# One selection made in two halves, message parts stored as floats, and a zero fill that waits for the loads

## The chip, the cores and the metric

The kernel runs on one core of one Trainium2 chip. The metric is the device time of one execution in microseconds. Three timed runs of the kernel before took 9149.21, 9165.05 and 9166.55 us; the median is 9165.05 us. The core has five engines that run side by side and wait for each other only through semaphores: TensorE (PE in the rows; PEld is its weight load), VectorE (DVE), ScalarE (ACT), GpSimd (POOL) and SyncE (SP), which here only issues DMAs.

## The reference

Four graph layers over 12500 nodes of 64 features and 400000 edges, `dst` sorted. Each layer's result is added to `x` and normalised over the features:

```python
x = ln(x + relu(segment_sum((x @ W0)[src] * edge_weight[:, None], dst)))
# layer 1: y = x + segment_sum over i=src of f(edge_attr) * (x @ Wl.T + bl)[dst]
#          f(e) = silu(e @ Wf1.T + bf1) @ Wf2.T + bf2 ; y = layernorm(y) * gamma + beta
x = ln(x + layer1(x))
# layer 2: h = x + segment_sum(x[src], dst); relu(h @ W1 + b1) @ W2 + b2
x = ln(x + layer2(x))
# layer 3: deg of src, dinv = rsqrt(deg); segment_sum over src of dinv[src]*dinv[dst]*(x @ W3)[dst] + bias
x = ln(x + layer3(x))
```

So every layer gathers a row per edge, makes a message of it, and sums the messages by node. The values are float32.

## The kernel before, in words

**Gather and scatter as matmuls.** Nodes are cut into 98 source blocks of 128 (NS) and 49 destination windows of 256 (NW). A cell is a pair of window and block, and holds up to 128 edges. For a cell a "hot" matrix (128 nodes x 128 edges) picks the rows of a node table, and a selection matrix (edges x 256 nodes of the window, or x 128 nodes of the block) sums the messages by node. Both are made on VectorE by comparing a row or a pair of indices with a ramp (`iotab`). A float is carried as three bfloat16 parts: the whole, the rest, and the low part; for a message they lie in three float slots, and the matmul reads the upper two bytes of each slot (`upper_half`).

**Stages, in order.** (1) A first block loads constants, weights and `x`; ACT issues the zero fill of the first four windows of the buffer `edge_rows` in DRAM (16 DMAs, L150); all engines meet at the end of the block. (2) `node_stage(0)` makes the first table. (3) `fused`, the longest stage, does two things at once: it computes the edge filter of layer 1 and writes one row per edge to its cell of `edge_rows`, and it runs layer 0 for a window whose cells are already sorted. (4) `node_stage(1)`, `filter_pass` (layer 1), (5) `node_stage(2)`, `sum_pass` (layer 2), (6) `node_stage(3)`, `read_pass` (layer 3), and the last normalisation. Other functions (`far_...`) are skipped at run time with these inputs.

**A beat of `fused`.** `run_beats` runs 52 beats (0 to 51). A beat has 14 steps (GW). In the beats 0 to 47 each of 13 steps also handles a chunk of 5 x 128 edges: DVE ranks the edges within their cells (`carried`, `ranked`, `placed`, `onehot`), PE does the filter matmuls and the counts, ACT writes the rows, and POOL scatters them with 5 indirect DMAs of 128 rows (L794): 65 in a beat, 3125 in all. Beats 49 to 51 have no chunks, and beat 48 has one. From beat 3 on each step also does the layer: `first` (hot matrix, L872), `second` (the selection of 7 cells x 256 nodes, L567, called at L880), on PE `gather` (L983) and `scatter` (L998), on ACT `whole` (L1070: table row times edge weight, straight into the first float slot), on DVE `remainder` (L887) and `lowest` (L892). The order within a step is written out by hand, once for each engine; buffers are double, and each wait names the step whose buffer comes free. SP loads the `piece` tiles of a window (f_piece) only when all indirect DMAs of the beat before have landed.

**`filter_pass`** goes through the windows in runs of 7 (98 runs), cut into sets of 2, 2, 2 and 1 windows. For each set DVE does `whole_message` (L1808, gathered row times filter), `first` (L1787), `rest_of_message` (L1819), `second` (L1796) and `low_of_message` (L1827). PE gathers the next set before it scatters this one (L1891, L1904).

Of the kernel before, what the change touches and what calls it, by code (L numbers as in the profile page):

```python
# [7 lines left out]
ALU = mybir.AluOpType  # L8
# [4 lines left out]
P = 128  # L13
# [48 lines left out]
def build(nc, a, out):  # L62
    ctx = ExitStack()
    with ctx:
# [87 lines left out]
        with nc.Block() as block:  # L152
# [13 lines left out]
            @block.scalar  # L166
            def _(act):
                act.wait_ge(s_const.sem, 12)
                for w in range(LEAD):
                    for q in range(4):  # L170
                        clear_quarter(act, w, q)
# [388 lines left out]
        def cells(g):  # L560

            return g // GH, g % GH * CG
# [14 lines left out]
        def fused():  # L577

            fctx = ExitStack()
            with fctx:  # L580
# [98 lines left out]
                with nc.Block() as block:  # L679
# [124 lines left out]
                    def _(dve):  # L804
# [70 lines left out]
                        def second(w, g):  # L875
                            h, lo = cells(g)
                            dma_wait(dve, y_pair[h], w)
                            wait(dve, y_sum, w, g - 1, GW)
                            settle(dve)
                            selection(dve, ysel[g % 2], ypair[h], lo, WIN).then_inc(y_sel.sem, 1)  # L880

                        def remainder(w, g):
                            wait(dve, y_whole, w, g + 1, GW)
# [5 lines left out]
                        def lowest(w, g):  # L889
                            wait(dve, y_rest, w, g + 1, GW)  # L890
                            settle(dve)
                            dve.tensor_tensor(upper_halves(msg[g % 2], 2), msg[g % 2][:, :, 1, :], upper_halves(msg[g % 2], 1),  # L892
                                              ALU.subtract).then_inc(y_low.sem, 1)

                        def summed(w):
# [6 lines left out]
                        def beat(b, extract, layer, prepare):  # L902
                            n = chunks(b)
                            more = chunks(b + 1) if isinstance(b, int) else BC
                            for g in range(GW):
# [15 lines left out]
                                if g < n:  # L921
                                    placed(b, g, 0)
                                    if g + 1 < n:
                                        onehot(b, g + 1)
                                if layer:
                                    lowest(b - 3, g)
                                if g < n:
# [779 lines left out]
        def filter_pass(n):  # L1707
# [3 lines left out]
            with ectx:  # L1711
# [21 lines left out]
                with nc.Block() as block:  # L1733
# [47 lines left out]
                    def _(dve):  # L1781
# [40 lines left out]
                        def low_of_message(t, s):  # L1822
                            lo, hi = steps(s)
                            part = msg[:, SETS[s][0] * CG:SETS[s][1] * CG, :]
                            reach(dve, x_rest, t, hi)
                            settle(dve)
                            dve.tensor_tensor(upper_of(part[:, :, 2 * D:3 * D]), part[:, :, D:2 * D],  # L1827
                                              upper_of(part[:, :, D:2 * D]), ALU.subtract).then_inc(x_msg.sem, hi - lo)

                        def run(t, i, last=False):  # L1830
# [549 lines left out]
```

## Time and profile before

| | us |
|---|---|
| median of three runs | 9165.05 |
| profiled execution, its own time | 9224.61 |
| its span | 9222.8 |
| PE / PEld busy | 7601.7 / 6594.3 |
| DVE busy | 6859.9 |
| ACT busy | 5230.8 |
| POOL busy | 3390.7 |

Rows are read so. In a table of windows: stretch, its length, then for each engine the busy time and the number of instructions, the granted share of TensorE's clock, the DMA share and GB/s. In a list of lines: line, engine, operation, out<-in by name, shape, count, then busy us and mean ns of one, then the idle time before it with what ended it. A timeline row is start, length, engine, line and names. In the waits: who waited for whom, the total, how many times, the longest. Records of one engine's successive instructions may overlap by some 0.1 us.

### The profile page before, as it was taken

To read this page: it belongs to the slowest core of one execution; us is meant where nothing else is said; L and a number is where in the kernel's file an instruction comes from. 1 tells how busy PE (TensorE), PEld (TensorE's weight loads), DVE (VectorE), ACT (ScalarE), POOL (GpSimd) and SP (SyncE) were. 2 spreads that over 40 slices of the span, in tenths; PEclk is the share of its full clock that TensorE was granted. 3 is DMA by queue.
4 is the path that set the end of the run, shared out by engine and by line. 5 is a ranking of instruction groups with operands and counts; after the bars stand their busy time and mean duration, and the time that the engine had idled before them with its cause. 6 is when DMAs were issued, how large, how long until landed. Compare 5 with 4: busy or idle time off the path is not lost. (4 is left out here: it accounts for less than half of the span.)

```text
span 9222.8 us, 312807 instructions
## 1 busy us (share of the span) xinstructions
PE 7601.7 (82%) x101781; PEld 6594.3 (72%) x101781; DVE 6859.9 (74%) x13109; ACT 5230.8 (57%) x12664; POOL 3390.7 (37%) x3201
## 2 busy tenths in 40 slices
PE   6688888888888888887577777776599998799998
PEld 3466666666666666665477777775599998799998
DVE  3476676766766667666689999998888887677777
ACT  2344444444444444444467777775577776688887
POOL 5777777777777777776000000000000000000000
PEclk8899999999999999998899999998799999899999
DMA  4555555555555555554277777774233332466665
GB/s 151 162 157 177 163 173 167 157 177 164 172 170 153 177 164 172 169 155 143 62 185 184 184 186 185 181 185 130 85 129 131 129 127 93 80 129 130 129 130 110
DMA packets 889994, 1385.03 MB, mean 150 GB/s; under 512 B 385510, under 2 KB 738726, under 8 KB 877174
## 3 DMA queue, kind: packets, MB, share of 16 engines
q1 hardware_dynamic: 760470, 1100.18, 44.2%
q10 hardware_dynamic: 29376, 174.02, 5.2%
q0 software_dynamic: 100000, 109.00, 4.0%
q8 instruction: 75, 1.23, 0.1%
q14 instruction: 73, 0.60, 0.0%
HBM read 1086.88 MB, written 295.86 MB: 150 GB/s over the span
## 5 line engine op out<-in xcount | busy, mean ns | idle before, releaser
L794 POOL DMA_INDIRECT edge_rows<-f_rows,f_index x3125 | 3290.9, 1053 | 967.2 <-issue 926.4
L1070 ACT ACTIVATE f_msg<-ps,f_yew 128x64 f32<-128x64 f32 x4802 | 1056.8, 324 | 1435.3 <-PE ps L983 1361.0
L567 DVE TENSOR_TENSOR x_sel<-iotab,x_pairs 128x1792 bf16<-128x1792 bf16 (+1 forms) x1372 | 1174.5, 856 | 208.1 <-issue 198.1
L1319 PE MATMUL ps<-x_msg,x_sel 128*128 128x192 bf16 x9604 | 1186.5, 246 | 2.5 <-issue 2.2
L1673 ACT ACTIVATE x_msg<-ps 128x384 bf16<-128x384 f32 (+1 forms) x2744 | 1015.3, 457 | 202.1 <-PE ps L1605 195.5
L1346 ACT ACTIVATE x_msg<-ps 128x768 bf16<-128x768 f32 (+1 forms) x1029 | 906.7, 916 | 353.5 <-PE ps L1300 303.2
L998 PE MATMUL ps<-f_msg,f_ysel 128*128 128x192 bf16 x9604 | 991.0, 256 | 108.9 <-issue 108.8
L1891 PE MATMUL ps<-tab,x_hot 128*128 (+1 forms) x28812 | 957.7, 194 | 23.5 <-ACT x_hot L1952 8.1
L1891 PEld LDWEIGHTS ps<-tab,x_hot 128*128 128x128 bf16 x28812 | 929.5, 98 | 53.7 <-issue 47.1
L998 PEld LDWEIGHTS ps<-f_msg,f_ysel 128*128 128x128 bf16 x9604 | 845.5, 99 | 135.7 <-issue 118.9
L1605 PE MATMUL ps<-tab,x_hot 128*128 (+1 forms) x9604 | 921.1, 247 | 18.8 <-ACT x_msg L1673 7.8
L1300 PE MATMUL ps<-tab,x_hot 128*128 128x192 bf16 x4802 | 790.2, 247 | 138.4 <-DVE x_hot L1249 138.4
L1952 ACT ACTIVATE x_hot<-x_away,ones 128x1792 bf16<-128x1792 bf16 (+1 forms) x392 | 628.4, 1603 | 400.0 <-PE ps L1891 382.0
L1319 PEld LDWEIGHTS ps<-x_msg,x_sel 128*128 128x128 bf16 x9604 | 831.3, 98 | 6.7 <-issue 3.3
L1605 PEld LDWEIGHTS ps<-tab,x_hot 128*128 128x128 bf16 x9604 | 799.8, 98 | 43.9 <-issue 26.4
L851 DVE TENSOR_REDUCE f_best<-ps 128x5 int32<-128x490 f32 x625 | 418.3, 669 | 503.0 <-PE ps L1025 498.6
L841 DVE TENSOR_SCALAR f_total<-ps 128x98 f32<-128x98 f32 x625 | 162.1, 259 | 835.4 <-PE ps L1013 828.9
L1904 PE MATMUL ps<-x_msg,x_sel 128*128 128x193 bf16 x4802 | 492.8, 251 | 348.3 <-issue 348.3
L1476 DVE TENSOR_SCALAR x_hot<-x_row,iota 128x896 bf16<-128x896 bf16 x1372 | 560.0, 451 | 277.9 <-PE ps L1605 258.1
L1860 POOL TENSOR_TENSOR x_added<-x_kept 128x448 f32<-128x448 f32 x14 | 18.5, 1323 | 2017.6 <-ACT x_kept L1964 2017.6
L567 DVE TENSOR_TENSOR f_ysel<-iotab,f_ypair 128x1792 bf16<-128x1792 bf16 x686 | 743.7, 1084 | 19.2 <-PE ps L998 12.7
L282 PE MATMUL ps<-bias_b,onesb 3*128 3x320 bf16 x625 | 196.1, 314 | 600.1 <-ACT f_hT L279 599.9
(190 smaller groups left out, 13971.7 us busy)
## 6 DMA issues: line engine op xcount, KB each, us to landing
x_row<-edge_row_dst SPq DMA_DIRECT2D x588, 448.0 KB, 4.9
edge_rows<-zeros ACTq DMA_DIRECT2D x204, 833.0 KB
f_piece<-edge_rows SPq DMA_DIRECT2D x343, 476.0 KB
f_yrow<-edge_row_src SPq DMA_DIRECT2D x686, 224.0 KB
x_row<-edge_row_src SPq DMA_DIRECT2D x98, 1568.0 KB, 6.3
x_f<-edge_rows SPq DMA_DIRECT2D x294, 476.0 KB, 3.7
edge_rows<-f_rows,f_index POOLq DMA_INDIRECT x3125, 2.3
x_row<-edge_row_dst SPq DMA_DIRECT2D x196, 224.0 KB, 3.4
```

The source lines that it names most:

```text
L567: return dve.tensor_tensor(sel[:, :, :].rearrange("p c (e two) -> p c e two", two=2), iotab[:, 0:columns].rearrange("p (e two) -> p e two" ...
L794: pool.indirect_dma_start(out=rowbuf, out_offset=bass.IndirectOffsetOnAxis(ap=index[:, j:j + 1], axis=0), in_=rows[:, j, :], in_offset=Non ...
L998: i = pe.matmul(sums[m], ysel[g % 2][:, c, m * P:(m + 1) * P], parts, start=False, stop=g == GW - 1 and c == CG - 1 and m == 1)
L1070: i = act.activation(msg[g % 2][:, c, 0, :], got[g % 2][:, c * D:(c + 1) * D], ACT.Copy, scale=yew[h][:, lo + c:lo + c + 1])
L1300: i = pe.matmul(psb[p % RING][:, k * VW:(k + 1) * VW], hot[c // CG % 2][:, c % CG, :], tab3[:, c, :, :].rearrange("p k d -> p (k d)"), sta ...
L1319: i = pe.matmul(total[:, m * VW:(m + 1) * VW], sel[c // CG % 2][:, c % CG, m * P:(m + 1) * P], msg[:, p % RING, k, :, :].rearrange("p k d ...
L1346: act.activation(msg[:, lo:hi, :, :, :].rearrange("p b k q d -> p b (k q d)"), psum[:, lo * 512:hi * 512].rearrange("p (b e) -> p b e", e= ...
L1476: o = dve.tensor_scalar(hot[BUFFER[j % RUN]][:, m, :, :].rearrange("p c e -> p (c e)"), row[h][:, at, :], iota2[:, m:m + 1], None, ALU.is_ ...
L1605: o = pe.matmul(got[k][:, c % 2 * VW:(c % 2 + 1) * VW], hot[b][:, m, c, :], piece(e, m * VW, VW), start=m == 0, stop=m == 1)
L1673: act.activation(msg[BUFFER[j]][:, 2 * k:2 * k + cells_of(k), :].rearrange("p c e -> p (c e)"), got[k][:, 0:cells_of(k) * VW], ACT.Copy).t ...
L1891: o = pe.matmul(psb[b][:, c * D:(c + 1) * D], hot[:, b, m, c * P:(c + 1) * P], piece(e + (j - lo) * WROW, m * VW + k * D, D), start=m == 0 ...
L1952: act.activation(hot[:, b:e, 1, :], away[:, 0:hi - lo, :], ACT.Relu, bias=ones[:, 0:1], scale=-1.0)\
```

## The change

Three edits.

1. The selection of 256 columns in `fused` becomes two instructions of 128 columns; the second stands behind `placed(b, g, 0)` and `onehot(b, g + 1)`, which so come between the halves. The semaphore is raised by the second.
2. In `lowest` and in `low_of_message` the third part is written as a float into its whole slot, not as a bfloat16 into the slot's upper half. The matmul reads the same upper half as before.
3. ACT's first 16 zero fills wait for the loads (`s_load`) and for the weight and bias blocks (`s_diag`).

```diff
             @block.scalar
             def _(act):
                 act.wait_ge(s_const.sem, 12)
+                act.wait_ge(s_load.sem, 16 * len(loads))
+                act.wait_ge(s_diag.sem, 16 * (len(blocks) + PARTS))
                 for w in range(LEAD):
                     for q in range(4):
                         clear_quarter(act, w, q)
...
                             wait(dve, y_sum, w, g - 1, GW)
                             settle(dve)
-                            selection(dve, ysel[g % 2], ypair[h], lo, WIN).then_inc(y_sel.sem, 1)
+                            chosen(w, g, 0)
+
+                        def chosen(w, g, m):
+                            h, lo = cells(g)
+                            shape = [P, CG, P // 2, 2]
+                            i = dve.tensor_tensor(ysel[g % 2][:, :, m * P:(m + 1) * P].rearrange("p c (e two) -> p c e two", two=2),
+                                                  iotab[:, m * P:(m + 1) * P].rearrange("p (e two) -> p e two", two=2)
+                                                  .unsqueeze(1).to_broadcast(shape),
+                                                  ypair[h][:, lo:lo + CG, :].unsqueeze(2).to_broadcast(shape), ALU.is_equal)
+                            if m == 1:
+                                i.then_inc(y_sel.sem, 1)
...
-                            dve.tensor_tensor(upper_halves(msg[g % 2], 2), msg[g % 2][:, :, 1, :], upper_halves(msg[g % 2], 1),
+                            dve.tensor_tensor(msg[g % 2][:, :, 2, :], msg[g % 2][:, :, 1, :], upper_halves(msg[g % 2], 1),
                                               ALU.subtract).then_inc(y_low.sem, 1)
...
                                     placed(b, g, 0)
                                     if g + 1 < n:
                                         onehot(b, g + 1)
+                                if go:
+                                    chosen(*ahead, 1)
                                 if layer:
                                     lowest(b - 3, g)
...
-                            dve.tensor_tensor(upper_of(part[:, :, 2 * D:3 * D]), part[:, :, D:2 * D],
+                            dve.tensor_tensor(part[:, :, 2 * D:3 * D], part[:, :, D:2 * D],
                                               upper_of(part[:, :, D:2 * D]), ALU.subtract).then_inc(x_msg.sem, hi - lo)
```

On DVE, a step of a beat in `fused` before: f_ysel is the selection, f_hot the one-hot of source blocks, f_msg the message, f_slot and f_index the placing.

```order
L851 TENSOR_REDUCE f_best<-ps 128x5
L898 TENSOR_REDUCE acc<-ps 128x2x64
L567 TENSOR_TENSOR f_ysel<-iotab,f_ypair 128x1792
L859 TENSOR_SCALAR f_slot<-f_best 128x5
L833 TENSOR_TENSOR f_hot<-iotas,f_src_block 128x490
L892 TENSOR_TENSOR f_msg<-f_msg 128x7x64
L865 SCALAR_TENSOR_TENSOR f_index<-f_slot,f_cell 128x5
L872 TENSOR_SCALAR f_yhot<-f_yrow,iota 128x896
```

The same step now.

```order
L853 TENSOR_REDUCE f_best<-ps 128x5
L910 TENSOR_REDUCE acc<-ps 128x2x64
L887 TENSOR_TENSOR f_ysel<-iotab,f_ypair 128x7x128
L861 TENSOR_SCALAR f_slot<-f_best 128x5
L835 TENSOR_TENSOR f_hot<-iotas,f_src_block 128x490
L887 TENSOR_TENSOR f_ysel<-iotab,f_ypair 128x7x128
L904 TENSOR_TENSOR f_msg<-f_msg 128x7x64
L867 SCALAR_TENSOR_TENSOR f_index<-f_slot,f_cell 128x5
L874 TENSOR_SCALAR f_yhot<-f_yrow,iota 128x896
```

The selection is in two, f_slot and f_hot stand between its halves, and the message's low part stands behind the second half. (The reduce into acc is there in a beat's first step alone.)

On ACT, the first block before, with what each instruction waits for.

```order
L150 DMA edge_rows<-zeros 128x1666 [waits s_const]
L150 DMA edge_rows<-zeros 128x1666 x15
L152 UNCONDITIONAL_BRANCH
L533 UNCONDITIONAL_BRANCH [waits barrier_Pool_Activation_PE_DVE_SP_release]
L368 ACT_TABLE_LOAD
```

And now.

```order
L150 DMA edge_rows<-zeros 128x1666 [waits s_diag,s_load,s_const]
L150 DMA edge_rows<-zeros 128x1666 x15
L152 UNCONDITIONAL_BRANCH
L535 UNCONDITIONAL_BRANCH [waits barrier_Pool_Activation_PE_DVE_SP_release]
L370 ACT_TABLE_LOAD
```

All 16 DMAs now stand behind the wait, and behind them stands the branch by which ACT leaves the block, and then the barrier that all engines pass before the node stage.

## Rows read from the trace of the kernel before

**Rows 1.** Table of windows: the start, fused with POOL, its tail, filter pass.

```profile
0.00:40.00 40.00, 0.08 (x1) 0.11 (x2) 2.79 (x13) 0.12 (x1) 11.17 (x23) 1.00 0.86 349
64.00:4334.00 4270.00, 3521.44 (x36786) 2671.16 (x36784) 2771.57 (x6979) 1797.57 (x7369) 3290.93 (x3126) 0.91 0.54 163
4334.00:4515.00 181.00, 107.44 (x1789) 101.34 (x1789) 138.69 (x226) 85.92 (x391) 0.15 (x1) 0.94 0.44 125
...
4625.00:6410.00 1785.00, 1393.47 (x33634) 1332.21 (x33631) 1678.13 (x1958) 1271.07 (x838) 54.41 (x41) 0.99 0.71 182
```

**Rows 2.** Waits of the whole span.

```profile
POOL edge_rows L794 <- issue: 926.4, 3040, 0.3
...
ACT f_mt L1107 <- DMA f_piece<-edge_rows: 683.7, 48, 53.0
```

**Rows 3.** POOL's indirect DMAs by line, 95 to 255 us (no layer yet).

```profile
L794 POOL DMA_INDIRECT edge_rows<-f_rows,f_index x127 | 123.4, 972 | 38.7 <-issue 37.8 <-ACT f_rows L1098 0.6 <-DVE f_index L865 0.3
```

**Rows 4.** The same, 605 to 4240 us (41 beats with a layer).

```profile
L794 POOL DMA_INDIRECT edge_rows<-f_rows,f_index x2666 | 2823.6, 1059 | 812.4 <-issue 793.5 <-DVE f_index L865 18.9
```

**Rows 5.** POOL's timeline, 2430 to 2438 us.

```profile
2430.53 0.96 POOL L794 DMA_INDIRECT edge_rows<-f_rows,f_index  x1 [0.30 <-issue]
2431.80 1.61 POOL L794 DMA_INDIRECT edge_rows<-f_rows,f_index  x1 [0.30 <-issue]
...
2435.09 1.18 POOL L794 DMA_INDIRECT edge_rows<-f_rows,f_index  x1 [0.30 <-issue]
```

**Rows 6.** DVE's timeline in the same stretch.

```profile
2431.50 1.08 DVE L567 TENSOR_TENSOR f_ysel<-iotab,f_ypair 128x1792 bf16<-128x1792 bf16 x1
...
2434.82 0.63 DVE L887 TENSOR_TENSOR f_msg<-f_msg 128x448 f32<-128x448 f32 x1
...
2436.75 1.08 DVE L567 TENSOR_TENSOR f_ysel<-iotab,f_ypair 128x1792 bf16<-128x1792 bf16 x1
```

**Rows 7.** DVE by line, 605 to 4240 us.

```profile
L567 DVE TENSOR_TENSOR f_ysel<-iotab,f_ypair 128x1792 bf16<-128x1792 bf16 x574 | 621.9, 1083 | 0.0
L892 DVE TENSOR_TENSOR f_msg<-f_msg 128x448 bf16<-128x448 f32 x574 | 378.0, 659 | 0.0
L887 DVE TENSOR_TENSOR f_msg<-f_msg 128x448 f32<-128x448 f32 x574 | 359.0, 625 | 6.3 <-PE ps L998 0.5
...
L872 DVE TENSOR_SCALAR f_yhot<-f_yrow,iota 128x896 bf16<-128x896 bf16 x574 | 269.8, 470 | 0.0
L833 DVE TENSOR_TENSOR f_hot<-iotas,f_src_block 128x490 bf16<-128x490 bf16 x533 | 219.4, 412 | 7.2 <-DVE f_early L825 7.2
```

**Rows 8.** DVE by line and shape, whole span: 128-column selection, parts of filter pass.

```profile
L567 DVE TENSOR_TENSOR x_sel<-iotab,x_pairs 128x896 bf16<-128x896 bf16 x686 | 425.3, 620 | 5.4 <-issue 3.9 <-PE ps L1615 1.5
...
L1827 DVE TENSOR_TENSOR x_msg<-x_msg 128x896 bf16<-128x896 f32 x294 | 375.3, 1277 | 0.0
...
L1819 DVE TENSOR_TENSOR x_msg<-x_msg 128x896 f32<-128x896 f32 x294 | 320.9, 1092 | 2.8 <-issue 2.6
L1808 DVE TENSOR_TENSOR x_msg<-ps,x_f 128x896 f32<-128x896 f32 x294 | 319.7, 1087 | 96.9 <-PE ps L1891 96.1 <-issue 0.8
```

**Rows 9.** Line L1827 alone: count, ns min/median/max, first and last start.

```profile
L1827 DVE TENSOR_TENSOR x_msg<-x_msg x392: 685/1234/2103, 4631.6 to 6404.4; 128x896 bf16<-128x896 f32 x196
```

**Rows 10.** Timeline of the start.

```profile
3.12 0.43 SPq L156 DMA_DIRECT2D x_rows<-in_x  x1
...
4.25 22.99 ACTq L150 DMA_DIRECT2D edge_rows<-zeros  x16
...
16.99 0.25 DVE L215 CAST bias_parts<-bias_rest 1x192 bf16<-1x192 f32 x1 [15.06 <-DMA x_rows<-in_x]
...
18.98 2.43 SPq L162 DMA_DIRECT2D bias_b<-bias_parts  x3
39.92 1.09 PE L365 MATMUL ps<-ident,x_rows 128*128 128x128 f32 x4 [39.92 <-PEq L152]
```

**Rows 11.** The zero fills' issue: count, ns min/median/max, first and last start.

```profile
L150 ACTq DMA_DIRECT2D edge_rows<-zeros x204: 338/343/6254, 4.2 to 4197.3; - x102
```

## The prediction, as put on record before the changed kernel ran

> **What bounds the kernel now.** I began with the table of windows [rows 1]: the fused stage with POOL's scatters takes 4270 us of 9222.8, the filter pass 1785. The pass over DVE's lines shows that the changed lines run in these two and in the 181 us tail of the fused stage, and the start is the fourth place.
>
> In the fused stage PE is busy 82% of the time, DVE 65%, POOL 77%. But the busy shares mislead: before 3040 of its 3125 indirect DMAs POOL sat idle for "issue" alone, 926.4 us in all and never more than 0.3 us at a time [rows 2]. So POOL ran one DMA after the other: 3290.9 us busy [rows 1] and 926.4 us of its own gaps are 4217 us of the 4270. The others wait for it: once in a window ACT waits for the `piece` load, which SP issues only when a beat's DMAs have landed, 683.7 us in 48 waits, so 14.2 us a beat [rows 2]. That is the slack that DVE, PE and ACT have in each beat. POOL alone sets the stage's end, and what I must cost is what the change does to POOL.
>
> An indirect DMA takes 972 ns on average in the beats without a layer [rows 3] and 1059 ns with one [rows 4]. Rows 5 and 6 tell why. The DMA that starts at 2431.80 takes 1.61 us and ends at 2433.41; the selection that was running on DVE ends at 2432.58, 0.83 us earlier. The one that starts at 2435.09 takes 1.18 us and ends at 2436.27; the L887 that was running ends at 2435.45, 0.82 us earlier. The one at 2430.53, with the selection starting only at 2431.50, takes 0.96 us. So a DMA that starts while one of these DVE instructions runs waits for its end and then needs 0.83 us; undisturbed it needs 0.96, so an instruction that ends less than 0.13 us after POOL's start costs nothing. L887 and L567 both read two tensors in SBUF.
>
> In the filter pass DVE is busy 1678 of 1785 us [rows 1], and its idle time is mainly 96.1 us for PE at L1808, about 1 us for each of the 98 runs [rows 8].
>
> **The selection in halves.** A POOL start at a random point of a step meets an instruction of length h with a chance that grows with h, and then waits (h - 0.13)/2 on average: together (h - 0.13)²/2. For one step the squares are, from rows 7: selection 1.083 us, 0.91; L892 0.659, 0.28; L887 0.625, 0.25; L872 0.470, 0.12; L833 0.412, 0.08; sum 1.64. A 128-column selection of this shape takes 620 ns [rows 8], so the two halves give 2 x 0.24 = 0.48, and the sum is 1.21: 26% less. POOL's waiting before is 3290.9 - 3125 x 0.96 = 291 us (0.96 being an undisturbed one), so about 76 us would go. The starts are not random: the step takes 5.25 us (from 2431.50 to 2436.75 in [rows 6]), and four DMAs with their gaps take 4 x (0.96 + 0.30) = 5.05 us. If POOL falls into step with DVE, it waits 0.2 us a step, whoever holds it up. This part does not shrink, so I take 65 us. The ends are a gain of 130 us (all steps without the long wait, double the estimate) and 0 (the waiting only changes its place). L892 as a float write loses at most 33 ns (659 against L887's 625), and this is 1% of the squares: nothing.
>
> The splitting's price on DVE: 2 x 620 against 1083 ns, 157 ns a step, less the 0.1 us by which records overlap, so 50 to 160 ns. In the beats with chunks it lies beneath the 14.2 us of slack a beat (14 x 0.16 = 2.2 us). In the tail nothing covers it: 181 us for some 56 steps, 3.2 us a step, with DVE busy 138.7 [rows 1], in a ring of DVE, PE and ACT. A ring over two steps has one selection pair and one L892: 56 x (0.05 to 0.16, less 0.03)/2 to the whole: 1 to 7 us, I take +3. The one-hot comes 0.46 us earlier for PE's counts (1.08 - 0.62), and the low part 0.05 to 0.13 us later for PE's scatter; both within the slack.
>
> The Trainium skill bears on this in "SBUF — State Buffer", section "SBUF: two separate sides". Its box on software-generated DMAs says that GpSimd can't write descriptors while DVE runs an instruction in a mode that uses both ports; a tensor_tensor is no such mode, and by the box alone the halves would change nothing on POOL (term 0, the second rival below). The list above it counts instructions with two SBUF inputs too, and the 1.61 us under the selection agrees with the list.
>
> **The low part as floats.** L1827 takes 1277 ns on average at 896 elements, and 1234 at the median [rows 8, 9]; its longest, 2.1 us, are few. L1819 has the same inputs in type and stride and writes floats: 1092 ns [rows 8]. Their difference to the typical one is 0.145 us. In a run the sets of two windows come three times (294 instructions in 98 runs), all in the ring DVE to PE to DVE; the single window's saving falls into the 1 us of idle time before L1808 and is worth nothing. So 294 x 0.145 = 43 us; a little is lost where POOL's own additions hold DVE up, so 42. Ends: 54 us (294 x 0.185, by the means) and 20 us (half of it given back as wait at L1808 for PE's gather, whose idle is there already).
>
> The skill's note on cachelines in the same section of the same page says that accesses within one 16-byte line go at full rate and that crossing costs. Floats and two-byte parts in float slots both make four accesses to a line, so by it the write would cost the same, and the term would be 0 (third rival). L1827 against L1819 disagrees, by 0.145 us.
>
> **The zero fill behind the loads.** Now ACT issues 16 DMAs of 833 KB from 4.25 us on, in 22.99 us, while `x` comes in; DVE gets its loads at 16.99 us, and the three bias DMAs issued from 18.98 us on land only with the end of the traffic, so PE starts at 39.92 [rows 10]; 349 GB/s over 40 us [rows 1]. Afterwards `x` (3.2 MB, issued at 3.12) has the engines to itself: at 349 GB/s and more, 9 us, so about 13 us. DVE's six small instructions take 2 us (16.99 to 18.98), the three issues up to 2.4 us, and a landing alone perhaps 2 us (an assumption; these rows show none in an idle queue): ACT is released at 19 to 20 us. Then it must issue 16 DMAs before it can leave the block. One takes 0.34 us at the median, 6.25 us at most [rows 11]: the queue holds a number of them and then takes one more per transfer of some 2 us. In the first stretch about 10 of 16 were outstanding at the end (the other traffic until 27.24 us leaves room for six transfers), so I expect six transfers, 12 us: the block ends at 32 us. That is -8. Ends: 19 + 16 x 0.34 = 24.4 us (-15), and 20 + 23 = 43 us with a second for SP (+4). The zeros (16 x 833 KB, 38 us at 349 GB/s) then drain beneath the node stage and are through at 58 us, before the fused stage at 64.
>
> **Sum.** -65 + 3 - 42 - 8 = -112 us. The profiled execution took 9224.61 us (span 9222.8) and would take 9112.6. The median of the runs is 59.6 us below the profiled one; I take the difference over to it: 9165.05 - 112 = 9053 us. The other terms' ends give 9053 + 65 + 4 + 22 + 12 = 9156 and 9053 - 65 - 2 - 12 - 7 = 8967 us.
>
> **Rivals.**
> - POOL keeps its waiting (gain of about 47 us). POOL locks to the step: 5.25 us against 5.05 for four DMAs, and the 0.2 us is waited at whichever instruction stands there. For it: the two numbers are that near. Against it: the mean wait is 0.099 us a DMA [rows 4], so 0.4 a step of four, not 0.2, and DMAs of 1.61 us are there [rows 5]. Time: 9165 + 3 - 42 - 8 = 9118 us. The skill's box above would lead to the same time.
> - The float write saves nothing, the rest comes: 9053 + 42 = 9095 us. For it only that L892 and L887, half as long, differ by just 33 ns; against it L1827 and L1819.
> - It gets slower: the two halves give POOL one more end per step to be caught at, with the one-hot between them. If a start per step is caught at the first half, and the next at the second or at L892, the waiting grows. 574 steps in 41 beats [rows 7] are 630 in 45 beats; with 0.3 us more in each that is +189 us: 9165 + 189 + 3 - 42 - 8 = 9307 us. It decides from 47/630 = 0.075 us more waiting a step, that is a mean DMA of 1059 + 19 = 1078 ns or more. Against it: two holds of 0.62 us have half the squared length of one of 1.08, and the longest single wait shrinks from 0.92 to under 0.5 us.
>
> **Chances.** Forecast 0.65 (its own range 9000 to 9095), POOL's waiting unchanged 0.17, float write of no use 0.07, slower by POOL 0.06, and 0.05 for gains beyond 8995. A measurement of this kernel can tell a change of about 0.2%, 18 us, from none. Faster by more than that: 0.65 + 0.05 + 0.07 and nearly all of 0.17, less 0.04 for an unforeseen give-back: 0.88; within: 0.05; slower: 0.07. The range of 8 in 10 goes from 8992 to 9128 us.
>
> **What would show it.** In the profile after: POOL's indirect DMA at a mean of about 1037 ns (65/2992 less) in the layer beats, the longest at 1.4 to 1.5 us in place of 1.88, and POOL's gaps still "issue" alone; the waits for f_piece a little shorter or the same; the fused stage with POOL at about 4197 us. L1827's successor at 1.09 us, and a filter pass of 1743 us. PE's first matmul at about 32 us. The tail at 184 us. It is wrong if POOL's mean stays above 1052 ns, if the filter pass gives its saving back as a longer wait at L1808, or if ACT's 16 issues take 23 us again.

## The result and the profile after

The changed kernel takes 9102.85 us (median of 4 runs, 9101.08 to 9115.69) against 9157.13 us for the kernel before (median of 4 runs: the three given above and one more); the ratio is 0.9945, with a 95% interval of 0.9932 to 0.9957. That is faster by 39 to 62 us, 50 in the middle. Forecast were 112 us and 9053 us. The time lies in the range of 8 in 10 (8992 to 9128 us), but less than half of the gain came.

The two profiles say something else: 9224.61 us before and 9115.69 after, 109 us apart, nearly the forecast. So the first thing to explain is that the profiled execution of the kernel before was 60 us slower than its timed ones, and that of the changed kernel only 13 us slower. Here are windows of the changed kernel (columns as in [rows 1]): the start, the fused stage with POOL's scatters, its tail, and the filter pass.

```profile
0.00:40.00 40.00, 0.00 (x0) 0.00 (x0) 2.79 (x13) 0.00 (x0) 11.15 (x23) 1.00 0.70 274
64.00:4257.00 4193.00, 3529.36 (x36789) 2674.77 (x36789) 2808.81 (x7614) 1793.00 (x7370) 3212.87 (x3126) 0.92 0.54 166
4257.00:4438.00 181.00, 105.92 (x1789) 100.08 (x1789) 141.28 (x274) 85.63 (x391) 0.30 (x1) 0.96 0.43 125
4549.00:6297.00 1748.00, 1392.91 (x33643) 1331.67 (x33640) 1636.58 (x1959) 1271.09 (x838) 52.69 (x41) 0.99 0.73 186
```

POOL's last scatter ends at 4257 us, 77 us earlier; the tail is nearly as long as it was (from the last scatter's end to the last selection's 174.4 us against 173.7); the filter pass is 37 us shorter; and the start gained nothing: PE has done nothing in the first 40 us. POOL's wait in the list of waits of the changed kernel, which answers to [rows 2]:

```profile
POOL edge_rows L796 <- issue: 950.3, 3117, 0.3
```

POOL still runs without a break but its own gaps. Its DMAs by line between 605 and 4150 us (compare [rows 4]):

```profile
L796 POOL DMA_INDIRECT edge_rows<-f_rows,f_index x2652 | 2737.3, 1032 | 808.5 <-issue 808.5
```

A DMA in the beats with a layer takes 1032 ns in place of 1059; 1037 was expected. The filter pass's parts by line and shape (compare [rows 8]), and the low part's line alone (compare [rows 9]):

```profile
L1841 DVE TENSOR_TENSOR x_msg<-x_msg 128x896 f32<-128x896 f32 x294 | 329.6, 1121 | 0.0
L1822 DVE TENSOR_TENSOR x_msg<-ps,x_f 128x896 f32<-128x896 f32 x294 | 319.3, 1086 | 106.3 <-PE ps L1905 105.1 <-issue 1.2
```

```profile
L1841 DVE TENSOR_TENSOR x_msg<-x_msg x392: 616/1083/1945, 4555.6 to 6291.7; 128x896 f32<-128x896 f32 x196
```

The low part takes 1083 ns in place of 1234 (medians), and the wait at L1822 grew by 9 us only. Now a step in DVE's timeline (start, us, engine, line, operation):

```profile
2407.65 0.62 DVE L887 TENSOR_TENSOR f_ysel<-iotab,f_ypair 128x896 bf16<-128x896 bf16 x1
...
2408.58 0.62 DVE L887 TENSOR_TENSOR f_ysel<-iotab,f_ypair 128x896 bf16<-128x896 bf16 x1
2409.12 0.61 DVE L904 TENSOR_TENSOR f_msg<-f_msg 128x448 f32<-128x448 f32 x1
...
2409.73 0.44 DVE L874 TENSOR_SCALAR f_yhot<-f_yrow,iota 128x896 bf16<-128x896 bf16 x1
```

and POOL's in the same stretch:

```profile
2408.54 0.96 POOL L796 DMA_INDIRECT edge_rows<-f_rows,f_index  x1 [0.31 <-issue]
2409.81 1.20 POOL L796 DMA_INDIRECT edge_rows<-f_rows,f_index  x1 [0.30 <-issue]
```

The DMA that starts at 2408.54, 0.04 us before the second half, is not held; the one at 2409.81 meets L874, which ends at 2410.17, and ends 0.84 us after it. The rule read from [rows 5, 6] holds here too, and this wait for DVE goes by no semaphore: beside the semaphores named at the start of this document it is a second way in which one engine holds up another.

Counted over the 3125 DMAs of each of the 14 profiles of this case, the rule has a sharp edge. Take the DMAs whose start falls into the selection, L887, L892, L833 or L872 (or the same instruction under its new line) with 0.19 us or more of it left. Of those that start 0.06 us or more after it began, 11965 of 11979 are held; of those that start less than 0.02 us after it began, 15 of 1350. Between the two, 669 are held and 582 are not. (Held is a DMA that takes 0.03 us or more beyond the 0.96.) L872 has one tensor input and holds as the others do. Of 3706 DMAs that fall so into the reductions from PSUM (L851 and L898) none is held.

### The profile page after: what moved, and what is told of

Read it like the earlier page. It is cut to its first block and busy times, and to the rows that moved or that the text cites. A ratio compares the mean times of both kernels' runs of the same rounds, so it can differ in the third digit from the quotient of the medians.

```text
span 9113.9 us, 313494 instructions
## 1 busy us (share of the span) xinstructions
PE 7609.2 (83%) x101781; PEld 6597.8 (72%) x101781; DVE 6856.6 (75%) x13795; ACT 5224.4 (57%) x12664; POOL 3311.2 (36%) x3201
## 3 DMA queue, kind: packets, MB, share of 16 engines
q8 instruction: 75, 1.23, 0.1%
## 5 line engine op out<-in xcount | busy, mean ns | idle before, releaser
L796 POOL DMA_INDIRECT edge_rows<-f_rows,f_index x3125 | 3213.0, 1028 | 967.6 <-issue 950.3
L887 DVE TENSOR_TENSOR f_ysel<-iotab,f_ypair 128x896 bf16<-128x896 bf16 x1372 | 838.3, 617 | 21.1 <-PE ps L1012 14.9
L1961 ACT ACTIVATE x_away<-x_row,upper_index 128x1792 bf16<-128x1792 bf16 (+1 forms) x392 | 628.4, 1603 | 49.4 <-DMA x_row<-edge_row_dst 8.1
```

Source lines behind the costliest of these rows:

```text
L796: pool.indirect_dma_start(out=rowbuf, out_offset=bass.IndirectOffsetOnAxis(ap=index[:, j:j + 1], axis=0), in_=rows[:, j, :], in_offset=Non ...
L887: i = dve.tensor_tensor(ysel[g % 2][:, :, m * P:(m + 1) * P].rearrange("p c (e two) -> p c e two", two=2), iotab[:, m * P:(m + 1) * P].rea ...
L1961: act.activation(away[:, 0:hi - lo, :], row[h][:, :, :], ACT.Abs, bias=upper_index[:, 0:1])\
```

## The experiments

All times are medians of timed executions; the ratio is to the kernel before, run beside it on the same chip, with its 95% interval. The base differs by round, so compare the ratios: it was 9160.23 us for "before again", the halves, both float writes and the zero fill; 9164.48 for the halves back to back, the quarters, the halves with one and with both float writes; and 9145.17, on another chip, for the rest of the experiments. "Scatters" is the stretch from the start of POOL's first to the end of its last indirect DMA in the profiled execution, "mean DMA" the mean of all 3125.

| kernel | us | ratio | scatters us | mean DMA ns |
|---|---|---|---|---|
| before, first profile | 9165.05 | | 4243 | 1053 |
| before again | 9160.36 | 1.0001 (0.9991 to 1.0010) | 4181 | 1033 |
| halves | 9123.67 | 0.9958 (0.9945 to 0.9972) | 4140 | 1020 |
| halves back to back | 9117.03 | 0.9946 (0.9933 to 0.9959) | 4136 | 1019 |
| quarters | 9131.48 | 0.9960 (0.9948 to 0.9972) | 4144 | 1021 |
| both float writes | 9114.96 | 0.9951 (0.9937 to 0.9964) | 4176 | 1031 |
| float write, fused stage | 9141.51 | 0.9995 (0.9986 to 1.0004) | 4167 | 1029 |
| zero fill behind the loads | 9158.75 | 0.9998 (0.9989 to 1.0008) | 4177 | 1032 |
| half the fill in the first block | 9149.87 | 1.0004 (0.9994 to 1.0013) | 4189 | 1036 |
| halves and filter pass's float write | 9086.73 | 0.9913 (0.9898 to 0.9927) | 4147 | 1022 |
| halves and both float writes | 9111.66 | 0.9944 (0.9931 to 0.9956) | 4164 | 1028 |
| the changed kernel (all) | 9102.85 | 0.9945 (0.9932 to 0.9957) | 4165 | 1028 |
| back to back, filter pass, half fill | 9079.67 | 0.9924 (0.9911 to 0.9938) | 4137 | 1019 |
| between, filter pass, half fill | 9080.35 | 0.9925 (0.9912 to 0.9939) | 4152 | 1024 |

**The kernel before once more.** No edit.

> The kernel before, unchanged, profiled and timed once more. In the first profile it took 9224.6 us, its timed executions 9149 to 9167; the changed kernel took 9115.7 in its profile and 9101 to 9104 otherwise. Theory A (GpSimd's lock-step with VectorE differs between executions or falls otherwise under the profiler): the profiled execution again lies 40 to 80 us above the timed ones, or at another value with a mean indirect DMA to match (10 ns of it are 31 us). Theory B (the first profile was one odd execution): profile and timed executions agree within 15 us, and the mean indirect DMA is 15 to 20 ns below the 1053 of the first profile.

The profiled execution took 9159.16 us, the timed ones 9139.28 to 9172.55. Theory B holds: the first profile was an odd execution. POOL's DMAs in the second profile, over the whole span and then by line from 605 to 4150 us:

```profile
L794 POOL DMA_INDIRECT edge_rows<-f_rows,f_index x3125: 954/958/1882, 91.7 to 4272.1; - x196
```

```profile
L794 POOL DMA_INDIRECT edge_rows<-f_rows,f_index x2644 | 2739.9, 1036 | 806.2 <-issue 750.7 <-DVE f_index L865 54.3 <-ACT f_rows L1098 1.2
```

And its window of the fused stage:

```profile
64.00:4273.00 4209.00, 3575.05 (x36786) 2704.29 (x36784) 2775.60 (x6979) 1793.81 (x7369) 3228.99 (x3126) 0.90 0.54 165
```

The longest DMA is the same 1882 ns, but the mean in the layer beats is 1036 ns, not 1059 [rows 4]. The filter pass agrees with the first profile within 2 us (1774 against 1775 us from first to last whole message), what follows it too, and the fused stage with the scatters is 61 us shorter. So nearly all of the difference of 65 us between the two executions is POOL's waiting for DVE. POOL waits 229 us here (3228.9 busy less 3125 x 0.96), not 291.

**The halves alone.**

```diff
-                            selection(dve, ysel[g % 2], ypair[h], lo, WIN).then_inc(y_sel.sem, 1)
+                            chosen(w, g, 0)
...
+                                if go:
+                                    chosen(*ahead, 1)
```

> Only the selection in two halves. By the prediction's terms (-65 for GpSimd, +3 tail): about 62 us faster, in profile and timing alike. Theory A (part of GpSimd's waiting before existed only under the profiler): 70 to 80 us faster by the profiles, but only 10 to 25 us faster by the timed executions, with the rest of the 54 us from the float writes. Theory C (the filter pass gives nothing in timed executions): about 50 us faster timed.

38 us faster (ratio 0.9958), and by the two later profiles 42 us in the scatters (4181 to 4140); the tail is 3 us longer (172.5 to 175.5 us to the last selection). Neither the 62 us of the prediction nor the 10 to 25 of theory A. Timing and profile agree once the base is the second profile. A stretch of POOL's timeline in this kernel:

```profile
2702.68 1.17 POOL L794 DMA_INDIRECT edge_rows<-f_rows,f_index  x1 [0.30 <-issue]
2704.15 0.96 POOL L794 DMA_INDIRECT edge_rows<-f_rows,f_index  x1 [0.30 <-issue]
2705.42 0.96 POOL L794 DMA_INDIRECT edge_rows<-f_rows,f_index  x1 [0.31 <-issue]
2706.68 0.96 POOL L794 DMA_INDIRECT edge_rows<-f_rows,f_index  x1 [0.30 <-issue]
2707.94 1.16 POOL L794 DMA_INDIRECT edge_rows<-f_rows,f_index  x1 [0.31 <-issue]
```

From 2702.68 to 2707.94 are 5.26 us, one step of DVE, in four DMAs of which one waits 0.2 us. This is the lock-step of the first rival. In such steps the halves give nothing. It is the usual step: counted in this trace from one L872 to the next, in the beats with chunks and a layer, a step takes 5.26 us and POOL waits 0.20 us in it (medians), and 297 of 373 steps with four DMAs have a wait between 0.1 and 0.3 us.

**Both float writes alone.**

```diff
-                            dve.tensor_tensor(upper_halves(msg[g % 2], 2), msg[g % 2][:, :, 1, :], upper_halves(msg[g % 2], 1),
+                            dve.tensor_tensor(msg[g % 2][:, :, 2, :], msg[g % 2][:, :, 1, :], upper_halves(msg[g % 2], 1),
...
-                            dve.tensor_tensor(upper_of(part[:, :, 2 * D:3 * D]), part[:, :, D:2 * D],
+                            dve.tensor_tensor(part[:, :, 2 * D:3 * D], part[:, :, D:2 * D],
```

> Only the low part written as floats, in the fused stage and in the filter pass. Theory A: 33 to 40 us faster, in profile and timing alike, since the filter pass has no indirect DMAs; filter pass 1739 us from its first to its last whole message against 1775.5. Theory C: 0 to 5 us faster in the timed executions.

45 us faster, a little more than expected. Theory C is out: the filter pass, 1742 us from its first to its last whole message against 1774, gives its gain in timed executions too. (In the eight profiles without this edit, the first one among them, the stretch takes 1768 to 1778 us, in the six with it 1738 to 1742.)

**The zero fill alone.**

```diff
                 act.wait_ge(s_const.sem, 12)
+                act.wait_ge(s_load.sem, 16 * len(loads))
+                act.wait_ge(s_diag.sem, 16 * (len(blocks) + PARTS))
```

> Only the first zero fill behind the loads. From the changed kernel's profile, where TensorE starts at 40.6 us against 39.9: within 2 us of the kernel before. The 16 issues from about 21.4 us on take 18.8 us. If GpSimd's phase against VectorE depends on where the start falls, the indirect DMAs' mean moves by more than 2 ns from the kernel before's; else it stays.

No change, 0.9998. The start of its timeline:

```profile
17.89 1.87 SPq L162 DMA_DIRECT2D bias_b<-bias_parts  x3
20.94 18.64 ACTq L150 DMA_DIRECT2D edge_rows<-zeros  x16
...
40.04 1.09 PE L367 MATMUL ps<-ident,x_rows 128*128 128x128 f32 x4 [40.04 <-PEq L152]
```

ACT was released at 20.9 us, 1 to 2 us later than predicted (19 to 20), but 16 issues took 18.6 us, 1.17 us each, so that the barrier opens at 40.0 us. The mean DMA of POOL stayed (1032 and 1033 ns).

The first four told that the parts, alone, are worth 38 + 45 + 0 us, and together 50. The four runs that follow are after the missing 33 us.

**Halves, and the float write in the filter pass alone.** The two edits of above, without the one in `lowest` and without the waits of the fill.

> The halves, and the float write in the filter pass alone; the fused stage's low part stays a bfloat16 and the zero fill stays early. Theory D (the effects add, and the float write in the fused stage costs the changed kernel part of the halves' gain by GpSimd's phase): 9160 - 37 - 33, so 9085 to 9095, with GpSimd's scatters at 4140 us from first to last start as with the halves alone. Theory E (there is a common limit for gains here, or the filter pass gives less timed): near the changed kernel's 9103.

80 us faster (0.9913, interval 68 to 93 us). Theory D holds: the halves' 38 and some 40 for the filter pass add.

**The changed kernel without the fill's waits.**

> The changed kernel without the waits before the first zero fill: halves and both float writes. Theory D: 9103 as the changed kernel, within 8 us, scatters at 4165 us. Theory F (the later start of the fill shifts GpSimd's phase and costs the 25 us): 9075 to 9085, scatters at 4140 us.

0.9944 against the changed kernel's 0.9945, scatters 4164 us: the fill has no part in it. (The time is 9 us above the changed kernel's, but its base is 7 us higher too.) So one edit stands between 0.9913 and 0.9944: beside the halves the float write in the fused stage costs 28 us (the intervals, 0.9898 to 0.9927 and 0.9931 to 0.9956, don't meet). POOL's timeline shows how. First the halves alone (in the fused stage they are the same kernel as the halves with the filter pass's float write), then this kernel, at the same place of the beat for the same window:

```profile
2055.98 1.22 POOL L794 DMA_INDIRECT edge_rows<-f_rows,f_index  x1 [0.30 <-issue]
2057.51 0.96 POOL L794 DMA_INDIRECT edge_rows<-f_rows,f_index  x1 [0.30 <-issue]
2058.77 0.96 POOL L794 DMA_INDIRECT edge_rows<-f_rows,f_index  x1 [0.30 <-issue]
2060.04 0.96 POOL L794 DMA_INDIRECT edge_rows<-f_rows,f_index  x1 [0.30 <-issue]
2061.30 1.09 POOL L794 DMA_INDIRECT edge_rows<-f_rows,f_index  x1 [0.30 <-issue]
2062.69 0.96 POOL L794 DMA_INDIRECT edge_rows<-f_rows,f_index  x1 [0.30 <-issue]
2063.95 0.96 POOL L794 DMA_INDIRECT edge_rows<-f_rows,f_index  x1 [0.30 <-issue]
2065.22 0.96 POOL L794 DMA_INDIRECT edge_rows<-f_rows,f_index  x1 [0.30 <-issue]
```

```profile
2064.40 1.20 POOL L794 DMA_INDIRECT edge_rows<-f_rows,f_index  x1 [0.30 <-issue]
2065.90 0.96 POOL L794 DMA_INDIRECT edge_rows<-f_rows,f_index  x1 [0.31 <-issue]
2067.16 0.95 POOL L794 DMA_INDIRECT edge_rows<-f_rows,f_index  x1 [0.30 <-issue]
2068.42 1.19 POOL L794 DMA_INDIRECT edge_rows<-f_rows,f_index  x1 [0.30 <-issue]
2069.91 1.20 POOL L794 DMA_INDIRECT edge_rows<-f_rows,f_index  x1 [0.30 <-issue]
2071.42 1.12 POOL L794 DMA_INDIRECT edge_rows<-f_rows,f_index  x1 [0.30 <-issue]
2072.85 0.96 POOL L794 DMA_INDIRECT edge_rows<-f_rows,f_index  x1 [0.30 <-issue]
2074.11 1.28 POOL L794 DMA_INDIRECT edge_rows<-f_rows,f_index  x1 [0.30 <-issue]
```

The one-hot in DVE's timeline of the first kernel:

```profile
2060.01 0.47 DVE L833 TENSOR_TENSOR f_hot<-iotas,f_src_block 128x490 bf16<-128x490 bf16 x1
```

And DVE's timeline in the second kernel:

```profile
2068.37 0.41 DVE L833 TENSOR_TENSOR f_hot<-iotas,f_src_block 128x490 bf16<-128x490 bf16 x1
2068.69 0.62 DVE L885 TENSOR_TENSOR f_ysel<-iotab,f_ypair 128x896 bf16<-128x896 bf16 x1
2069.23 0.62 DVE L902 TENSOR_TENSOR f_msg<-f_msg 128x448 f32<-128x448 f32 x1
...
2069.84 0.45 DVE L872 TENSOR_SCALAR f_yhot<-f_yrow,iota 128x896 bf16<-128x896 bf16 x1
...
2071.09 0.62 DVE L897 TENSOR_TENSOR f_msg<-f_msg 128x448 f32<-128x448 f32 x1
...
2073.95 0.62 DVE L885 TENSOR_TENSOR f_ysel<-iotab,f_ypair 128x896 bf16<-128x896 bf16 x1
```

Both begin alike: held once, then two DMAs of 0.95 or 0.96 us. In the second kernel the fourth starts at 2068.42, 0.05 us after the one-hot L833, and is held until 0.83 us past that one's end. From there each start but one meets a holder: L872 (until 2070.29), L897 (until 2071.71), the second half of the next selection (until 2074.57). In the first kernel the fourth starts at 2060.04, 0.03 us after its one-hot, and is not held: the two lie on either side of the edge counted above; only one of the later four is. Eight DMAs with their gaps take 10.50 us in the first kernel (2055.98 to 2066.48, the last row's 0.96 and a gap of 0.30 added) and 11.29 in the second (2064.40 to 2075.69). The instruction that was changed is 0.04 us shorter (653 to 617 ns by their lines); what differs is where POOL's starts fall. Over the whole stage the profiles show 17 us of it in the scatters (4147 against 4164), the timed executions 25 us between the medians and 28 between the ratios. The stretch alone doesn't show that this place is typical for all of it. The count over all 3125 DMAs of the two profiles does: with the float write in the filter pass alone 833 DMAs are held for more than 0.05 us and the waits add up to 201 us, with both float writes 902 and 218 us. Of the 17 us, DMAs that fall into the selection wait 16 us more, into L872 6 more, into the one-hot 4 more, and into L897 and L902, the shortened one, 10 less. How far such a sum is a matter of the single execution the two kernels with the same fused stage tell, the halves alone and those with the filter pass's float write: 7 us (4140 and 4147).

**The halves back to back.**

```diff
+                            chosen(w, g, 0)
+                            chosen(w, g, 1)
```

> The kernel before with the selection in two halves back to back, the placing work behind both. Theory G (what counts is the length for which one instruction holds GpSimd up): 30 to 40 us faster, as with the placing between; longest indirect DMA about 1.4 us. Theory H (what counts is the earlier placing and one-hot, or where the gaps lie): 0 to 10 us faster or slower.

49 us faster, more than the 30 to 40 expected; the longest DMA is 1488 ns. Theory H is out. Theory G fits: the placing between the halves brings nothing, and could as well have stayed behind them. That the length of one instruction is what counts holds only down to the halves, as the next run shows.

**Quarters.**

```diff
+                            Q = P // 2
+                            shape = [P, CG, Q // 2, 2]
...
+                                if go:
+                                    chosen(*ahead, 1)
+                                if g < n and g + 1 < n:
+                                    onehot(b, g + 1)
+                                if go:
+                                    chosen(*ahead, 2)
+                                    chosen(*ahead, 3)
```

> The kernel before with the selection in four instructions of 64 columns, f_slot behind the first and f_hot behind the second. A quarter should take 0.39 us (0.62 less half of the 0.46 by which 1.08 lies above 0.62), four of them 0.47 us more than one whole, which is still within VectorE's slack in the beats with chunks. By the square law (sum of (h - 0.13) squared: 1.21 with halves, 0.27 + 0.73 = 1.00 with quarters) GpSimd would wait 35 us less than with halves, and the tail costs 56 x 0.2 = 10 us more: 15 to 25 us faster than the halves alone, 9100 to 9108. Theory A (lock-step, in which 0.2 us are waited in each step whoever holds): the same as the halves or up to 15 us slower, 9120 to 9140.

As theory A says: a quarter takes 386 ns as expected, but the mean DMA (1021 ns) is that of the halves (1020), and the tail is 9 us longer (184.1 against 175.5 us to its last selection). The square law promised 35 us that did not come. POOL's waiting has a floor that is not a matter of the holders' lengths: counted as above, 248 of 346 steps with four DMAs wait between 0.1 and 0.3 us. The quarters even raise it. They make DVE's step 5.30 us long in place of 5.26, and the wait in a step is 0.23 us in place of 0.20 (medians); four DMAs with their gaps take 5.05.

The last four take the start apart, put the good parts together, and run the fused stage's float write alone.

**Half of the zero fill in the first block.** With the waits; ACT issues the other 8 DMAs at the head of the fused stage.

```diff
-                for w in range(LEAD):
+                for w in range(LEAD // 2):
...
+                        for w in range(LEAD // 2, LEAD):
+                            for q in range(4):
+                                clear_quarter(act, w, q)
                         run_beats(act, beat)
```

> The kernel before with the first zero fill behind the loads, and only 8 of its 16 DMAs issued in the first block, the other 8 by ScalarE at the head of the fused stage. If the start term failed on the rate of issue (1.17 us each, back to back, whatever the transfers do), ScalarE is free at 21.4 + 8 x 1.17 = 31 us and TensorE starts there, 9 us earlier than before; the time falls by 5 to 9 us if the fused stage's first loads come earlier with it. If it failed on the queue's depth (no more DMAs are taken while transfers run), the first 8 go out in 3 to 4 us and TensorE starts at 25 us.

The rate of issue was it: 8 DMAs take 8.35 us, and PE starts at 30.2 us. But the gain is given back at once: 1.0004.

The start of its timeline, all engines:

```profile
21.39 8.35 ACTq L150 DMA_DIRECT2D edge_rows<-zeros  x8
...
30.20 1.09 PE L367 MATMUL ps<-ident,x_rows 128*128 128x128 f32 x4 [30.20 <-PEq L152]
```

SP's timeline at the head of the fused stage, then POOL's:

```profile
69.40 5.15 SPq L694 DMA_DIRECT2D f_ea<-in_ea  x4
```

```profile
94.63 1.19 POOL L796 DMA_INDIRECT edge_rows<-f_rows,f_index  x1 [26.35 <-ACT f_rows L1100]
```

For comparison, the same two in the first profile of the kernel before:

```profile
77.19 2.16 SPq L692 DMA_DIRECT2D f_ea<-in_ea  x4
```

```profile
91.34 1.19 POOL L794 DMA_INDIRECT edge_rows<-f_rows,f_index  x1 [15.27 <-ACT f_rows L1098]
```

The loads of f_ea are issued 7.8 us earlier, but in 5.15 us in place of 2.16, and from the start of their issue to POOL's first scatter it is 25.2 us in place of 14.2. So it is in all profiles: 13.3 to 14.5 us in the eleven with the whole fill in the first block, 25.0 to 25.2 in the three with half of it. The 10 us won at the start are lost here. The other 8 zero fills, which ACT issues from 68.61 us on, are in flight beside these loads; that they slow them is the likely cause, but no run shows it apart. Timed, nothing is left of the 10 us.

**The parts that gain, together.** Halves back to back, or with the placing between; float write in the filter pass alone; half of the fill.

> Halves back to back, the float write in the filter pass alone, and the half zero fill in the first block. If the gains add (47 for the halves back to back, 33 for the filter pass, 5 to 9 for the start): 9072 to 9080 us. If GpSimd's phase takes part of it back: 9085 to 9095.

> The same with the placing between the halves, as in the changed kernel. 9086.7 of the halves with the filter pass, less 5 to 9 for the start: 9078 to 9082 us. It tells with the run beside it whether the place of the second half matters: theory G says no (within 8 us).

69 us (57 to 81) and 69 us (56 to 81) faster: both ahead of the changed kernel by their middle values, though the intervals overlap (0.9932 to 0.9957 there), and neither ahead of the halves with the filter pass's float write alone (0.9913, 9086.7 us). The two times, 9080 us, look like the sums that were expected, but the base of this round is 9145 us, not 9160: the gains fell short of the 78 to 89 us that the sums meant. The place of the second half does not matter.

**The float write in the fused stage alone.**

> The float write in the fused stage alone. The instruction gets some 40 ns shorter (0.65 to 0.615 us). Theory D (its sign depends on where it makes GpSimd's starts fall): beside the whole selection 5 to 12 us faster, as the difference between both float writes (45) and the filter pass (33) says, while beside the halves it cost 17 to 25 us. A theory in which a float write in itself harms the fused stage would have it 15 us or more slower here too.

No change that can be told (0.9995, up to 13 us faster). So the same edit does nothing beside the whole selection and costs 28 us beside the halves. The 5 to 12 us that theory D gave it are not told from none. It is no cost of the instruction, and by the count above it is where POOL's starts fall.

## Why the prediction was wrong, step by step

Forecast were 65 us for the halves, less 3 for the tail, 42 for the filter pass, nothing for L892 and 8 for the start: 112. The experiments give in their place 38 us for the halves with their tail, some 42 for the filter pass (80 less 38), 28 lost by L892, and nothing for the start: 52 us, and 50 were measured. So three terms failed. L892 was put at nothing and cost 28 us; the halves with their tail were put at 62 us and gave 38; the start was put at 8 us and gave none. The next paragraphs take them one by one.

**What bounds the kernel: right.** POOL sets the fused stage, and its waiting for DVE is what the halves change. In all 14 profiles no gap between two of POOL's scatters is longer than 0.35 us. The 0.83 us rule holds in them, with the edge that the prediction had not seen: a DMA that starts within 0.02 us of the holder's start goes free, and one that starts 0.06 us after it is held.

**"The median of the runs is 59.6 us below the profiled one; I take the difference over": wrong.** I had the sign of trouble in hand and took it for a constant of profiling. It was the state of the very quantity that I was pricing: in the profiled execution POOL waited 291 us, in the second profile, as long as the timed runs, 229. The changed kernel has 213 (3213.0 less 3125 x 0.96). By the prediction's own law this step is worth 16 us (26% of the 62 between 291 and 229), less than L892. From profile to profile the forecast of 112 met 109 by luck, and so did the sign that was given for it, a mean DMA of 1037 ns in the layer beats (1032 measured): three terms were off, and the odd execution made up for them. That the time lies in the stated range is owed to the range's width; it lies between the first two rivals (9118 and 9095 us), but what they said did not come: POOL's waiting fell, and the float write in the filter pass gave its 42 us.

**The halves, -65 us: the mechanism right, the size off.** They give 38 us alone (49 back to back). The square law (26% of the waiting) would give 60 us from the 229 of the second profile; the profile shows 42. The rest is the floor: in steps of 5.25 us four DMAs wait 0.2 us, whoever holds. The prediction named this as a rival and took 11 us off for it (76 less 65); it was worth 11 to 22 (60 less 49 or 38), and more in quarters, where waiting fell no further. The prediction's own numbers could have told that the law does not fit. By it POOL waits 1.64/2 for a start each 1.36 us (1.059 + 0.30), so 0.60 us a step and 380 us in 630 steps, and 291 and 229 were measured; 0.2 us in each of 630 steps are 126 us that cannot shrink.

**L892 as a float write, "nothing": wrong beside the halves.** I priced its length and not what a shift of 0.04 us does to a pattern of starts: 28 us back. The edge makes such a shift count: 0.03 us after the one-hot a DMA goes free, 0.05 us after it it waits. Without this edit the kernel would be at 0.9913.

**The tail, +3 us: right.** 172.5 to 175.5 us with the halves alone.

**The low part in the filter pass, -42 us: right.** L1841 at 1.083 us in place of 1.234, and the stretch from the first to the last whole message 35 us shorter; timed, both float writes give 45 us and the one in the fused stage 4. The give-back at L1822 was 9 us: 294 x (1.277 - 1.121) less 9 are 37, the difference of the two windows. By the Trainium skill's note on cachelines ("SBUF — State Buffer", "SBUF: two separate sides") there would have been no difference; for two-byte writes into four-byte slots the measurement decides against it.

**The start, -8 us: wrong.** ACT's release came 1 to 2 us later than predicted (20.9 us; in the changed kernel 21.4). But I read the 22.99 us of 16 issues as a full queue that drains by transfers, and from the 0.34 us median that a free queue takes DMAs fast. Issued back to back behind the loads they take 1.17 us each, so 18.6 us. (The 23 us that were to be the sign of this term's failure did not come either; 18.75 in the changed kernel were enough.) And even the 10 us that the half fill won at the start were lost in front of POOL's first scatter.

**The rival of slower POOL: did not come.** The timelines and the halves' 38 us show that a tensor_tensor holds POOL up. The box in the Trainium skill's "SBUF — State Buffer", "SBUF: two separate sides", names only instructions in a mode that uses both ports, and would have given 0. The list above it also counts instructions with two SBUF inputs, which agrees with the runs; but it counts them only against a GpSimd op that reads SBUF, a condition that the prediction left out and that no run here tests.

Left open: why the execution of the first profile fell into the pattern with 291 us and kept it for 40 beats (87.4 to 89.0 us, most of them 88.7), while the second profile moves among beats of 85.3 to 89.1 us. The edge is part of it: in the second profile 187 DMAs start within 0.04 us of the one-hot's start and go free, in the first 42. No run here steers the phase by itself, so that it decides is shown by counting in the traces, not by an edit of its own.

## What to carry to other kernels

When the profiled execution is further from the timed ones than these are from each other, profile once more before a sum is made against it: the difference may be the very term. When two engines run periodic work and one holds the other up, length of the holder sets a bound only; beyond it the phase decides (here the place of 0.04 us), effects need not add, and an edit that is free by its length can cost more than it could ever save. Test such edits one by one, and keep those that gain beside the others.

## What the runs showed of the hardware that was not expected

- An indirect DMA of POOL that starts while DVE runs the selection, a message part (L887, L892), the one-hot (L833) or the hot matrix (L872, one tensor input) ends 0.79 to 0.84 us after it (98 in 100 of the 11965 held ones), whatever its own start; undisturbed it takes 0.96 us. It is held if it starts 0.06 us or more after the instruction did (11965 of 11979), and not if it starts less than 0.02 us after it (15 of 1350 held). Under reductions from PSUM none of 3706 is held. The longest took 1.88 us under a 1.08 us selection, and 1.49 to 1.53 us with halves of 0.62 us; these last are a little more than the rule gives (0.62 + 0.83 = 1.45), and why stays open.
- A tensor_tensor that writes bfloat16 into the upper halves of float slots takes 1.23 us at 128 x 896, the same that writes floats 1.08 to 1.09 us (medians).
- DMAs of 833 KB issued back to back by ACT behind the loads take 1.17 us each to issue (16 in 18.64 us; 8 in 8.35 us), a single one 0.34 us.
- A tensor_tensor on bfloat16 takes 1.08, 0.62 and 0.39 us for 1792, 896 and 448 elements a partition.
